# Selective-scan kernel: the carried states copied by ScalarE in place of VectorE

## What is computed

```python
h = exp(delta[:, :, None] * A) * h + (delta * x)[:, :, None] * B[:, None, :]
y = einsum('ben,bn->be', h, C)
```

## Time and profile before

| what | value |
|---|---|
| median of 3 runs | 1269.93 us |
| the profiled execution: its own time | 1272.05 us |
| its span in the trace | 1270.2 us |
| mean granted PE clock | 0.929 |
| busy: PE, DVE, ACT, POOL | 1076.9, 1173.1, 1010.5, 998.2 us |

### The profile page before, as it was taken

The page is one execution under the profiler, slowest core; times in us unless marked ns, Lnnn a source line. Parts: engine busy times, 40 slices in busy tenths (PEclk is TensorE's granted clock), DMA queues, the critical chain, the costliest instruction groups (busy, mean ns, idle before and its releaser), DMA issues.

```text
span 1270.2 us, 20047 instructions
## 1 busy us (share of the span) xinstructions
PE 1076.9 (85%) x5406; PEld 806.6 (64%) x5406; DVE 1173.1 (92%) x2128; ACT 1010.5 (80%) x2151; POOL 998.2 (79%) x601
## 2 busy tenths in 40 slices
PE   4378576498898989999999999999999999998776
PEld 3266475365666666676767766676766667675664
DVE  5976899989999899999999999999999999999896
ACT  4898346379888897889888898889889898987853
POOL 1487176667898988889898998889899898988764
PEclk8686778798999999999999999999999999998977
DMA  7467822644445454555545454555545455544536
GB/s 229 154 200 227 312 82 82 203 162 130 142 141 153 135 148 153 145 149 137 149 133 161 134 161 139 147 148 131 155 139 157 142 150 150 147 134 132 135 128 191
DMA packets 87117, 195.08 MB, mean 154 GB/s; under 512 B 11184, under 2 KB 47152, under 8 KB 86928
## 3 DMA queue, kind: packets, MB, share of 16 engines
q1 hardware_dynamic: 69008, 171.18, 40.7%
q0 software_dynamic: 17712, 22.55, 10.9%
q10 hardware_dynamic: 288, 0.07, 0.0%
HBM read 171.22 MB, written 26.48 MB: 156 GB/s over the span
## 4 chain that ended last, share of the span: by engine, by line
PE 31%; POOL 29%; ACT 14%; issue 13%; DVE 11%; DMA 1%; POOLq 0%; DVEq 0%; ACTq 0%
POOL part L775 15%; PE yps L870 7%; POOL acc L831 5%; POOL tap L805 4%; ACT aexp L557 4%; PE bankX L1067 4%; PE bankH L1033 4%; PE bankV L1057 4%; DVE hb L1170 3%; PE bankG L910 3%; POOL scr L783 2%; ACT L557 2%; DVE bps L1149 2%; PE bankV L910 2%; POOL x L807 2%
## 5 line engine op out<-in xcount | busy, mean ns | idle before, releaser
L775 POOL TENSOR_TENSOR part<-hb,bcr 128x1024 f32<-128x1024 f32 x256 | 618.3, 2429 | 172.4 <-DVE hb L1170 141.2
L1170 DVE TENSOR_TENSOR_SCAN hb<-aexp,carry,bps 128x256 f32<-128x256 f32 x768 | 545.5, 734 | 4.2 <-ACT aexp L557 4.1
L557 ACT ACTIVATE aexp<-delta,Am 128x256 f32<-128x256 f32 x1024 | 446.8, 501 | 53.0 <-DVE hb L1170 42.0
L870 PE MATMUL yps<-idn,part 128*128 128x128 f32 x2048 | 299.8, 286 | 74.1 <-POOL part L775 64.0
L1149 DVE TENSOR_TENSOR bps<-ups,bcr 128x512 f32<-128x512 f32 x512 | 345.8, 675 | 3.4 <-DMA bcr<-brows 2.3
L870 PEld LDWEIGHTS yps<-idn,part 128*128 128x128 f32 x2048 | 249.9, 147 | 151.2 <-POOL part L775 83.0
L1170 DVE TENSOR_TENSOR_SCAN hb<-aexp,bps 128x256 f32<-128x256 f32 x256 | 167.3, 673 | 10.8 <-ACT aexp L557 10.2
L1067 PE MATMUL bankX<-w,scr 128*128 x568 | 138.7, 388 | 10.5 <-ACT scr L715 8.1
L1033 PE MATMUL bankH<-w,scr 128*128 x284 | 136.8, 604 | 2.2 <-issue 1.0
L1057 PE MATMUL bankV<-v,scr 128*128 x284 | 134.2, 595 | 1.2 <-ACT xin L610 0.8
L831 POOL DMA_INDIRECT acc<-scr,idx x71 | 114.2, 1609 | 24.6 <-issue 11.5
(11 more groups left out here) (179 smaller groups left out, 1625.1 us busy)
## 6 DMA issues: line engine op xcount, KB each, us to landing
bcr<-brows SPq DMA_DIRECT2D x256, 512.0 KB
w<-in_W SPq DMA_DIRECT2D x2, 4096.0 KB, 22.1
xch<-in_x SPq DMA_DIRECT2D x16, 256.0 KB, 4.5
w<-in_x SPq DMA_DIRECT2D x4, 1024.0 KB, 9.7
xt<-scr SPq DMA_DIRECT2D x16, 256.0 KB, 3.0
acc<-scr SPq DMA_DIRECT2D x16, 256.0 KB, 2.8
v<-in_V SPq DMA_DIRECT2D x1, 4096.0 KB, 16.0
acc<-mst POOLq DMA_DIRECT2D x15, 256.0 KB
```

The lines of the kernel that those rows point to most:

```text
L557: nc.scalar.activation(aexp[:, w % EXP_SLOTS, i, :], delta[:, c % 2, e, :], ACT.Exp, scale=Am[:, e, n:n + 1]).then_inc(s_a, 1)
L775: nc.gpsimd.tensor_tensor(part[:, slot:slot + 2, :, :], hb[:, state:state + 2, :, :], bcr[:, row:row + 2, CH:2 * CH].unsqueeze(2).to_broad ...
L870: mm = pe.matmul(yps[:, s, i * P:(i + 1) * P], part[:, w % (2 * PART_PAIRS), i, s * P:(s + 1) * P], idn[:, :], start=(n == 0 and s == 0 an ...
L1170: v.tensor_tensor_scan(hb[:, w % STATE_SLOTS, i, :], aexp[:, w % EXP_SLOTS, i, :], bps[w % 2][:, i, :], first, ALU.mult, ALU.add).then_inc ...
```

## The change

The function moves from the DVE queue to the ACT queue, at the same units, and its instruction becomes an ACTIVATE with Copy. The semaphore counts and who waits for them stay as they are.

```diff
@@ ACT @@
+            def keep_carry(w):
+
+                c, q, n = unit(w)
+                if carried(c):
+                    act.wait_ge(s_scan, 2 * (w + 1) + 2)
+                    slot = w % STATE_SLOTS
+                    nc.scalar.activation(carry[:, q, n:n + 2, :], hb[:, slot:slot + 2, :, CH - 1], ACT.Copy).then_inc(s_cc, 1)
...
             for w in range(UNITS):
+                if w % 2 == 1 and w >= 3:
+                    keep_carry(w - 3)
                 if w + EXP_AHEAD < UNITS:
                     exps(w + EXP_AHEAD)
@@ DVE @@
-            def keep_carry(w):
-
-                c, q, n = unit(w)
-                if carried(c):
-                    dve.wait_ge(s_scan, 2 * (w + 1) + 2)
-                    slot = w % STATE_SLOTS
-                    v.tensor_reduce(carry[:, q, n:n + 2, :], hb[:, slot:slot + 2, :, CH - 1:CH], AX.X, ALU.max).then_inc(s_cc, 1)
...
             for w in range(UNITS):
-                if w % 2 == 1 and w >= 3:
-                    keep_carry(w - 3)
                 scan(w, 0)
```

## The result

The changed kernel took 1267.46 us in the median of 11 runs (1265.33 to 1269.51), the kernel before 1270.24 in the same set; the ratio is 0.9971 (95% interval 0.9962 to 0.998). In a second set it was 1267.11 against 1270.84, ratio 0.9965 (0.9954 to 0.9977). So it is faster by 0.3%, some 3 to 4 us, a little more than a measurement of this kernel can tell from no change. The forecast was 0.3 us.

The account below looks back on a forecast made before the run. No single engine bounds it: DVE is busiest, but the chain runs through POOL, PE and ACT, DVE leading in chunk 1. DVE saves 3.5 us, ACT adds 3.2, net -0.3: 1269.6 us, range 1264.5 to 1274.5.

Parts of the forecast that it names:

- The prices: Queue cost per copy, from start to start: 0.055 us saved on DVE, 0.10 us added on ACT.
- ACT's side: Copies that fall where ACT holds the chain of waits, in chunks 0 to 14: 3.2 us added in total.
- Rival 2: DVE bounds throughout; eight chunks with copies and carried scans give back 0.88 us each: 1264.2 us; chance 0.20, part included.
- Rival 3: The copy on ACT brings table loads of 1.28 us; one per chunk adds 15 us, so 1285; chance 0.01.
- The reading of chunks 7 and 11: Same work as chunks 6 and 10 without copies: taking all 16 off DVE is worth some 0.47 us a chunk.
- The 2.5 copies of chunk 1: ACT's stretch on the chain in chunk 1, 208 to 226.5 us, holds 2.5 copies, taken as three: 0.3 us added.
- DVE's 0.88: The most DVE can gain per chunk, in us; chunk 1 was to gain nearly all of it, 0.8.
- The terms of chunks 5, 6, 9, 10 and 13: DVE saves 1.4 us in 6, 10 and 13, 0.9 in 5 and 9; ACT adds one copy, 0.10, in each.
- Chunk 0's 1.3 us: 13 of 16 copies fall into ACT's stretch on the chain in chunk 0: 1.3 us added, nothing gained on DVE.
- The 0.3 of chunks 8 and 12: ACT holds the chain there for three copies at 0.10 us: 0.3 us added a chunk, nothing gained on DVE.
- rival 1: ACT paces the mixed chunks and becomes slower, at the tanh and bankX evictions: 1273.0 to 1276.5 us; chance 0.24.

Follow-up runs that it names:

- the kernel with both: Against the kernel before: DVE keeps its reduction into carry and ACT also makes the copy, into a spare tile; 1273.72 us, ratio 1.0018.
- the control: The changed kernel once more, unedited, in the set of follow-up runs; 1267.11 us against 1270.84 for the kernel before.

## Why the prediction was right and wrong

The terms of the sum, against the means of four traces of before and three of the change, in us:

| chunks | forecast | measured |
|---|---|---|
| 0 | +1.3 | +0.5, with 1.5 to 1.8 us of scatter in either kernel |
| 1 | -0.5 | -0.9 |
| 2, 3, 4 | +0.2 | -1.3 |
| 5, 6, 9, 10, 13 | -1.8 | -2.0 |
| 8, 12 | +0.6 | +0.3 |
| 7, 11 | 0 | -0.1 |
| 14, 15 | -0.1 | -1.4 |
| sum | -0.3 | -4.9 |

The measured time lies in the range of the forecast, but a kernel faster by over 0.2%, which is what came, had been given a chance of 0.20. That the time came so near is not the merit of the sum, in which one term was missing and others erred.

With the stretches before chunk 0 and after chunk 15 the spans differ by 4.7; the medians of the timed runs differ by 2.8 and 3.7.

- **The prices were right.** 0.055 us on DVE and 0.10 on ACT, by reading start to start: the median distance from a copy to the next start is 51 ns on DVE before and 98 ns on ACT after. That ACT's side in total (3.2 forecast, 2.3 to 2.9 in the kernel with both) agrees is luck in part, since 1.5 us of chunk 15 are taken off the measured figure. Rival 2, DVE's whole slot, fell: with no copies anywhere the gain was 6.0, not 10.6. Rival 3 fell: 50 table loads stand at the exponentials as before.
- **The reading of chunks 7 and 11 was right** as a measure of the chunks that resemble them: chunk 6 without copies took 72.22, 0.53 less, against 0.47.
- **The 2.5 copies of chunk 1, "taken as three: 0.3"**, failed. Chunk 1 took 119.0 with and without ACT's copies. ACT idles for 65 us there, and the chunk collected all of DVE's 0.88.
- **The terms of chunks 5, 6, 9, 10 and 13 came out by luck in part.** The mean of -2.0 holds the one trace of the change in which chunk 9 had no drop of the clock (70.71). By the medians of the traces the five give -1.4: 0.3 in chunks 6 and 10 and 0.2 in chunk 13, where the net forecast was 0.37 each, 0.5 in chunk 5 and 0.1 in chunk 9.
- **Chunks 2 to 4 decide nothing.** Their mean fell by 1.3, and the kernel with no copies took 217.95 us there against a mean of 219.46. But one of the four traces of before took 217.63, less than any of the change (218.0 to 218.2), and in two of the other three chunk 3 had a drop of the clock that no trace of the change has there (72.7 against 71.6).
- **Chunk 0's 1.3 us is shown by no trace.** The kernel with no copies took 86.97 there, more than any trace of before, so the scatter hides a term of this size. The 0.3 of chunks 8 and 12 was 0.1 to 0.2.
- **Chunk 15 was not in the sum at all**, since nothing changes in it. It gave 1.6 of the 4.9. This is the main miss: the sum held only terms at the place of the edit, and took the stretches without a copy at nothing without a reason.
- The direction was open in the forecast and the size small, which the range covered. That rival 1 stayed away was luck to a degree: with the cost on ACT doubled it arrived, at 1275.5, where the linear sum would have given 1270.

## What to carry to other kernels

Price a small instruction by the distance of starts, not by its recorded duration: here 139 ns were 51, and 202 were 98. Where an edit moves 0.1 us at a time between two loaded engines, measure each side alone and then doubled: the second dose on ACT cost some three times the first. Totals of such kernels add up only if a stretch that changed in all of them is set apart. And look outside the edited stretch, at the clock of PE too: chunk 15, which was not edited, gave more than any chunk that was.

## What was unexpected in the hardware

One short drop of the clock goes with over a microsecond. Chunk 9 of the changed kernel, with the drop (granted clock 0.98) and, in the control's trace, without it:

```profile
752.62:824.77 72.15, 66.62 (x330) 48.00 (x329) 69.08 (x111) 63.48 (x150) 62.28 (x37) 0.98 0.52 146
```

```profile
753.71:824.42 70.71, 64.91 (x330) 46.84 (x329) 68.86 (x112) 63.67 (x150) 61.76 (x37) 1.00 0.51 143
```

The same kernel, the same work, 1.4 us apart. The matmuls of `bankX` that fall into the drop, and DVE's product behind them, first with the drop and then without:

```profile
813.40 2.87 PE L1077 MATMUL bankX<-w,scr 128*128 x8
821.54 0.69 DVE L1350 TENSOR_TENSOR scr<-scr,bankV 128x512 f32<-128x512 f32 x1 [1.05 <-PE bankV L1067]
```

```profile
814.11 1.89 PE L1077 MATMUL bankX<-w,scr 128*128 x8
821.19 0.69 DVE L1350 TENSOR_TENSOR scr<-scr,bankV 128x512 f32<-128x512 f32 x1
```

So 1.05 us of the 1.4 are one wait behind the drop; 0.3 were lost some 20 us before it. PE had stood idle for 2.5 us ahead of it in both traces, and the clock fell in one. Chunk 3 of the kernel before agrees: 71.6 us in two traces without a drop, 72.7 in two with one. Such drops come in some executions and not in others, here in chunks 3, 4, 5 and 9, which have five expert tiles. They fit the spread of 5.5 to 6.5 us between runs of the kernel before in the sets of 14, 20 and 24 runs: in the set of 24, the four longest had a mean granted clock of 0.923 to 0.924, the four shortest 0.930 to 0.933.

A DMA of 512 pieces of 4 bytes, 192 times (the page counts 112560 packets under 512 B, 11184 before), was nearly no burden: chunks 8 and 12 took what they took with no copies at all (71.96 and 71.98 against 71.98 and 71.97), chunks 6 and 10 took 0.2 us more, and one load of rows on the same queue was 7.2 us in the issuing.
